# Masks on VectorE, reciprocals left in PSUM and keys copied by ScalarE in the first attention of a two-layer transformer kernel

## The chip, the cores and the metric
One core of one Trainium2 chip runs the whole program. The metric is device time in microseconds (us) of one execution. Engines: PE is TensorE, DVE is VectorE, ACT is ScalarE, POOL is GpSimd, SP is SyncE; PSUM is the memory that TensorE writes, in banks of 128 partitions by 512 fp32 elements, and SBUF the memory of everything else.

## The reference, cut to what matters
The program is two pre-norm transformer layers over x of shape (2, 512, 512). The change touches only the first attention:

```python
x = x + _L0_attn_ref(_layernorm(x), Wq, Wk, Wv, Wo)    # 32 query heads, 8 key/value heads, head size 16
x = x + _L0_ffn_ref(_layernorm(x), ...)
x = x + _L1_attn_ref(_layernorm(x), ...)               # 32 query heads, 8 key/value heads, head size 128
x = x + _L1_ffn_ref(_layernorm(x), ...)

# inside _L0_attn_ref
scores = einsum('bhqd,bhkd->bhqk', q, k_h) / math.sqrt(HEAD_DIM)
scores = where(causal, finfo.min, scores)
attn = softmax(scores, axis=-1)
ctx = einsum('bhqk,bhkd->bhqd', attn, v_h)
return ctx.transpose(0, 2, 1, 3).reshape(b, t, D_OUT) @ Wo
```

## The kernel before, in words
`program` runs stages one after the other: the projection of the first attention (`project0`), the first attention itself (`attend0`), the first feed forward, the second attention (`attention1`), the second feed forward. In each stage every engine has its own program, written out by hand, and executes it strictly in order; engines wait for each other through counting semaphores.

`attend0` (from L1036) works through 8 units u. A unit is one batch and one pair of key/value heads x = 0, 1 with their HPG = 4 query heads each. In a unit there are four query tiles i = 0 to 3 of 128 queries, which see (i + 1) * 128 keys. The softmax is computed in two passes over the scores.

- **First pass, the maxima.** `scores` (L1158) puts scores of 4, 2, 1 and 1 heads into one PSUM bank for i = 0, 1, 2 and 3 (`S_BANKS = [1, 2, 4, 4]` banks for each x). For each head there is one matmul (L1170), and then one bf16 matmul of the identity with the mask (L1173) adds -1e30 to what lies above the diagonal. Three banks go round (`claim_score` waits for `score_read`). On DVE, `maxima` (L1365) takes the negated row maximum of each bank with a `tensor_reduce` (L1369). `put_maxima` splits the maxima of a query tile into two parts and writes them beside the queries (L1381, L1383). The one-head banks, i = 2 and i = 3, are 16 in a unit and 128 in all.
- **Second pass, the weights.** The queries, now with their maxima, are turned by PE (`turn_queries` with again = 1, L1155) and copied out by DVE (`read_queries`, L1405). `turned_scores` (L1187, with its own mask matmul L1190 on the diagonal) gives keys by queries for four heads at once, minus the maximum; ACT takes the exponential (`exponentials`, L1564) and rounds it to its high part (`high`, L1573); POOL subtracts to get the low part (L1683); `weigh` (L1202, L1203) multiplies both with the values, which carry a column of ones for the row sums, into `cbank`. This is done 20 times in a unit, 160 times in all.
- **Out.** DVE copies `cbank` out (`read_heads`, L1414), PE turns it back into `hbank` (`turn_back`, L1208 on, matmuls L1215), and `take_heads` (L1416) on DVE takes the reciprocals of the row sums into the SBUF tile `rsum` (L1424), copies one half of the result (L1425), adds the other (L1427) and multiplies with the reciprocals (L1432). This is done 32 times. `turn_tile` and `project_tile` make the output projection, in the last units and the tail.
- **Keys.** For each unit PE turns four key tiles into `qkbank` (`turn_keys`, L1139) and DVE copies the two halves of partitions, 64 x 512 each, into `k_rows` (`read_keys`, L1393 and L1394). Its place in the order of DVE is between `read_heads(u, 1)` and `take_heads(u, 1)`. `qkbank` is shared by turned keys, turned queries and turned output tiles, one after the other.

On PE, the order of a unit mixes `scores` of unit u with `turned_scores` and `weigh` of unit u - 1. `turn_keys(u)` stands near the start, then come `weigh`, `turn_back`, `turned_scores` and two `weigh`, then `scores(u, 0, 0, 0)`, which needs the keys. The order on ACT at that place is two `exponentials`, then `high(u, 2, 0, 2)`.

The second attention already has the helper `masked_maximum` (L227). It is one DVE operation that adds the mask from SBUF to the scores in PSUM, writes them back and accumulates the minimum of their negative; in the trace it is two instructions, the operation itself and a read of the accumulator, both at L230:

```python
def masked_maximum(nc, m, bank, n, to):
    scores = bank[:, 0:n]
    return nc.vector.tensor_tensor_reduce(scores, scores, m.mask_w[:, T - n:T], -1.0, LARGE, ALU.add, ALU.min, to)
```

`mask_w` is 128 x 512, zero but for its last 128 columns. The memset that makes these zeros (L1466, the third to signal `zeroed`) stands in `attend0` already.

Of the kernel before, what the change touches and what calls it, by code (L numbers as in the profile page):

```python
# [17 lines left out]
ACT = mybir.ActivationFunctionType  # L18
AX_X = mybir.AxisListType.X

P = 128
# [3 lines left out]
QT = T // P  # L25
NG, HPG = 8, 4
HD0, HD1 = 16, 128
# [1008 lines left out]
def attend0(nc, m, inp):  # L1036
# [4 lines left out]
    X2 = 2  # L1041

    S_BANKS = [1, 2, 4, 4]
    M_ALL = X2 * J_ALL
# [10 lines left out]
    def live(u):  # L1055

        return 0 <= u < NU

    done = m.hand_over()
    with ExitStack() as ctx:  # L1060
# [7 lines left out]
        prob = sb("prob", [P, NE, 512])  # L1068
        p_hi, p_lo = sb("p_hi", [P, NP, 512], F32R), sb("p_lo", [P, NP, 512], F32R)
        head_t = m.raw[:, 4:6, :]  # L1070
        rsum, head_sum = sb("rsum", [P, 2, HPG, X2]), sb("head_sum", [P, HPG, X2, HD0])
        head = sb("head", [P, NT, NG * HPG, HD0])
        raw_wo = head[:, QT:NT, :, :].rearrange("p t h n -> p t (h n)")
        c_hi, c_lo = sb("c_hi", [P, 2, KT, P], F32R), sb("c_lo", [P, 2, KT, P], F32R)
# [37 lines left out]
        def _(pe):  # L1112
# [45 lines left out]
            def scores(u, i, x, bank):  # L1158
                if not live(u):
                    return  # L1160
                per, n = HPG // S_BANKS[i], (i + 1) * P
                if x == 0 and bank == 0:
                    pe.wait_ge(q_read, QT * u + i + 1)
                    if i == 0:
                        pe.wait_ge(keys_read, 2 * (u + 1))
                        if u == 0:
                            pe.wait_ge(zeroed, 2)
                out = claim_score()
                for h in range(per):
                    nc.tensor.matmul(out[:, h * n:(h + 1) * n], q_rows[:, bank * per + h, :], k_rows[:, u % 2, x, 0:n],  # L1170
                                     start=(h == 0), stop=False)
                diagonal = out[:, 0:per * n].rearrange("p (h n) -> p h n", h=per)[:, :, i * P:n]
                nc.tensor.matmul(diagonal, m.ident_b[:, :], m.mask_b[:, :].unsqueeze(1).to_broadcast([P, per, P]),  # L1173
                                 start=False, stop=True).then_inc(scored, 1)
                scored_by[QT * u + i] = count["score"]

            def turned_scores(u, i, x, j):

# [27 lines left out]
            def turn_back(u, i):  # L1206

                if not live(u):  # L1208
                    return
                n = QT * u + i  # L1210
                pe.wait_ge(c_read, n + 1)
                if n >= 1:
                    pe.wait_ge(divided, 3 * n)
                for h in range(HPG):
                    last = nc.tensor.transpose(hbank[:, h * VX:(h + 1) * VX], head_t[0:VX, n % 2, h * P:(h + 1) * P],  # L1215
                                               m.ident[0:VX, 0:VX])
                last.then_inc(backed, 1)
# [138 lines left out]
        def _(dve):  # L1356
# [8 lines left out]
            def maxima(u, i, x, bank):  # L1365
                if not live(u):
                    return
                per, n = HPG // S_BANKS[i], (i + 1) * P
                nc.vector.tensor_reduce(nmax[:, i % 2, bank * per:(bank + 1) * per, x],  # L1369
                                        next_score()[:, 0:per * n].rearrange("p (h n) -> p h n", h=per),  # L1370
                                        AX_X, ALU.max, negate=True).then_inc(score_read, 1)

            def put_maxima(u, i):
# [7 lines left out]
                nc.vector.tensor_copy(heads[:, :, 0], both).then_inc(parted, 1)  # L1381
                dve.wait_ge(parted, 2 * n + 1)
                nc.vector.tensor_tensor(heads[:, :, 1], both, heads[:, :, 0].bitcast(F32), ALU.subtract).then_inc(parted, 1)  # L1383

            def read_keys(u):
                if not live(u):
                    return
                dve.wait_ge(keys_turned, u + 1)
                if u >= 2:
                    dve.wait_ge(t_scored, M_ALL * (u - 1))  # L1390
                elif u == 0:
                    dve.wait_ge(zeroed, 2)
                nc.vector.tensor_copy(k_rows[0:64, u % 2, 0, :], qkbank[0:64, :]).then_inc(keys_read, 1)  # L1393
                nc.vector.tensor_copy(k_rows[64:P, u % 2, 1, :], qkbank[64:P, :]).then_inc(keys_read, 1)  # L1394

            def read_queries(u, i):

# [18 lines left out]
            def take_heads(u, i):  # L1416

                if not live(u):
                    return
                n, t, at = QT * u + i, (u // PAIRS) * QT + i, X2 * HPG * (u % PAIRS)  # L1420
                view = hbank[:, 0:HPG * VX].rearrange("p (h x n) -> p h x n", h=HPG, x=X2)
                s, r = head_sum[:, :, :, :], rsum[:, n % 2, :, :]
                dve.wait_ge(backed, n + 1)
                nc.vector.reciprocal(r, view[:, :, :, HD0]).then_inc(divided, 1)  # L1424
                nc.vector.tensor_copy(s, view[:, :, :, V1:VW]).then_inc(divided, 1)  # L1425
                dve.wait_ge(divided, 3 * n + 2)
                nc.vector.tensor_tensor(s, view[:, :, :, 0:HD0], s, ALU.add).then_inc(divided, 1)  # L1427
                dve.wait_ge(divided, 3 * n + 3)
                if u == PAIRS and i == 0:
                    dve.wait_ge(wo_ready, KT)  # L1430
                to = head[:, t, at:at + X2 * HPG, :].rearrange("p (x h) n -> p h x n", x=X2)
                nc.vector.tensor_tensor(to, s, r.unsqueeze(3).to_broadcast([P, HPG, X2, HD0]), ALU.mult).then_inc(head_ready, 1)  # L1432
# [34 lines left out]
            for u in range(-1, NU + 1):  # L1467
                first = 2 * (u - PAIRS - 1) if u in (PAIRS + 1, PAIRS + 2) else None
                tail = u == NU
                maxima(u, 1, 0, 1)  # L1470
                maxima(u, 1, 1, 0)
                maxima(u, 1, 1, 1)
                put_maxima(u, 1)
                if u == NU - 1:
                    dve.wait_ge(stats_made, QT)
                    next_ln.variances(dve)
                maxima(u, 2, 0, 0)
                maxima(u, 2, 0, 1)
                if first is not None:
                    low(first)  # L1480
                maxima(u, 2, 0, 2)
                maxima(u, 2, 0, 3)
                if tail:
                    low(QT)
                take_heads(u - 1, 2)
                if tail:
                    add_tile(QT)
                    low_row(2)
                    make_row(3)
                    low(QT + 1)  # L1490
                    add_tile(QT + 1)
                    low_row(3)
                    low(QT + 2)
                read_queries(u, 1)
                maxima(u, 2, 1, 0)
                maxima(u, 2, 1, 1)
                maxima(u, 2, 1, 2)
                maxima(u, 2, 1, 3)
                put_maxima(u, 2)
                if first is not None:  # L1500
                    add_tile(first)
                if u == NU - 1:
                    next_ln.inverses(dve)
                    make_row(0)
                maxima(u, 3, 0, 0)
                maxima(u, 3, 0, 1)
                if first is not None:
                    low(first + 1)
                maxima(u, 3, 0, 2)
                maxima(u, 3, 0, 3)  # L1510
                read_heads(u - 1, 3)
                read_queries(u, 2)
                if u == NU - 1:
                    low_row(0)
                    make_row(1)
                maxima(u, 3, 1, 0)
                take_heads(u - 1, 3)
                if tail:
                    add_tile(QT + 2)
                    low(QT + 3)  # L1520
                    low_rank_low()
                    add_tile(QT + 3)
                read_heads(u, 0)
                maxima(u, 3, 1, 1)
                maxima(u, 3, 1, 2)
                maxima(u, 3, 1, 3)
                put_maxima(u, 3)
                if first is not None:
                    add_tile(first + 1)
                if u == NU - 1:  # L1530
                    low_row(1)
                    make_row(2)
                take_heads(u, 0)
                read_queries(u, 3)
                read_heads(u, 1)
                read_keys(u + 1)
                take_heads(u, 1)
                maxima(u + 1, 0, 0, 0)
                maxima(u + 1, 0, 1, 0)
                put_maxima(u + 1, 0)  # L1540
                maxima(u + 1, 1, 0, 0)
                read_heads(u, 2)
                read_queries(u + 1, 0)

        @block.scalar
        def _(act):
            def read_queries(u, i):
                if not live(u):
                    return
                n = QT * u + i  # L1550
# [52 lines left out]
            for u in range(-1, NU + 1):  # L1603
# [40 lines left out]
                high(u, 2, 1, 1)  # L1644
                exponentials(u, 2, 0, 2)
                exponentials(u, 2, 1, 2)
                high(u, 2, 0, 2)
                exponentials(u, 3, 0, 0)
                high(u, 2, 1, 2)
# [847 lines left out]
```

## Time and profile before
| | |
|---|---|
| three runs | 1460.55, 1460.55, 1463.03 us (median 1460.55) |
| profiled execution | 1460.84 us, of which 1459.0 us are the span of the instructions |
| mean granted TensorE clock | 0.985 |
| busy share of the span | PE 93%, DVE 70%, ACT 50%, POOL 47% |
| `attend0` in the profile | from about 71.8 to 372.7 us |
| its keys are turned (L1139) from | 73.3, 108.4, 137.6, 167.1, 196.7, 226.3, 265.6 and 305.1 us |

The last line gives the edges of the units. Busy time of PE is a union of matmuls whose ends are modelled and overlap: a matmul of 512 columns is shown with 0.39 us, while one follows the other every 0.23 us. What an instruction costs in a dense stream is thus read from the distance of the ends (start plus duration) of neighbours, not from its duration. In rows of the timeline the first two numbers are start and duration in us, and a bracket gives the idle time of the engine before it and what ended it.

### The profile page before, as it was taken

To read this page: it belongs to the slowest core of one execution; us is meant where nothing else is said; L and a number is where in the kernel's file an instruction comes from. 1 tells how busy PE (TensorE), PEld (TensorE's weight loads), DVE (VectorE), ACT (ScalarE), POOL (GpSimd) and SP (SyncE) were. 2 spreads that over 40 slices of the span, in tenths; PEclk is the share of its full clock that TensorE was granted. 3 is DMA by queue.
4 is the path that set the end of the run, shared out by engine and by line. 5 is a ranking of instruction groups with operands and counts; after the bars stand their busy time and mean duration, and the time that the engine had idled before them with its cause. 6 is when DMAs were issued, how large, how long until landed. Compare 5 with 4: busy or idle time off the path is not lost. (4 is left out here: it accounts for less than half of the span.)

```text
span 1459.0 us, 20197 instructions
## 1 busy us (share of the span) xinstructions
PE 1359.1 (93%) x6904; PEld 1086.5 (74%) x6904; DVE 1020.4 (70%) x2063; ACT 726.4 (50%) x1574; POOL 685.4 (47%) x533
## 2 busy tenths in 40 slices
PE   4779999988898699999999999999999999699999
PEld 3656666655576588888888888888888887578887
DVE  6769998785757677778777787778877878532322
ACT  2548887676534355444544454545544454243332
POOL 3548887666363544244433543444424431055453
PEclk9989999999999999999999999999999999999999
DMA  3000000100110211011110110101101010043332
GB/s 108 3 28 1 1 1 1 25 6 15 52 36 1 73 30 44 9 36 30 29 38 8 37 37 16 44 15 30 44 15 30 22 44 1 15 107 83 103 93 82
DMA packets 64933, 50.72 MB, mean 35 GB/s; under 512 B 5760, under 2 KB 54272, under 8 KB 64576
## 3 DMA queue, kind: packets, MB, share of 16 engines
q1 hardware_dynamic: 64832, 49.43, 11.9%
q8 instruction: 56, 0.92, 0.3%
q14 instruction: 45, 0.37, 0.1%
HBM read 47.32 MB, written 2.10 MB: 34 GB/s over the span
## 5 line engine op out<-in xcount | busy, mean ns | idle before, releaser
L1683 POOL TENSOR_TENSOR a_p_lo<-a_prob,a_p_hi 128x512 fp32r<-128x512 f32 x160 | 203.8, 1288 | 86.3 <-ACT a_p_hi L1573 84.4
L695 ACT ACTIVATE a_pt_hi<-a_ring 128x512 fp32r<-128x512 f32 x160 | 93.8, 596 | 175.8 <-PE a_ring L402 175.7
L831 POOL TENSOR_TENSOR a_rot_a<-a_rot_a,a_rot_b 128x512 f32<-128x512 f32 x80 | 103.5, 1294 | 139.1 <-DVE a_rot_b L574 139.1
L686 ACT ACTIVATE a_prob<-a_score,a_nmax 128x128 f32<-128x128 f32 (+3 forms) x256 | 132.0, 529 | 57.4 <-DVE a_nmax L539 29.0
L2296 POOL TENSOR_TENSOR f_w_lo<-raw,f_w_hi 128x512 fp32r<-128x512 f32 (+2 forms) x66 | 90.8, 1402 | 142.4 <-ACT f_w_hi L2239 142.3
L340 PE MATMUL a_xo<-h_hi,a_w_hi 128*128 128x512 f32 x384 | 151.2, 394 | 5.3 <-POOL a_w_lo L841 4.2
L342 PE MATMUL a_xo<-h_hi,a_w_lo 128*128 128x512 f32 x384 | 151.1, 393 | 0.0
L341 PE MATMUL a_xo<-h_lo,a_w_hi 128*128 128x512 f32 x384 | 150.4, 392 | 0.0
L836 POOL TENSOR_TENSOR a_p_lo<-a_rot_a,a_p_hi 128x512 fp32r<-128x512 f32 x80 | 103.3, 1292 | 69.4 <-ACT a_p_hi L712 69.4
L556 DVE TENSOR_TENSOR a_pt_lo<-a_ring,a_pt_hi 128x512 fp32r<-128x512 f32 x160 | 108.5, 686 | 33.1 <-ACT a_pt_hi L695 32.1
L1573 ACT ACTIVATE a_p_hi<-a_prob 128x512 fp32r<-128x512 f32 x160 | 99.7, 629 | 45.0 <-PE a_cbank L1203 43.0
L1369 DVE TENSOR_REDUCE a_nmax<-a_score 128x1 f32<-128x512 f32 (+3 forms) x176 | 104.6, 634 | 17.3 <-PE a_score L1173 17.1
L841 POOL TENSOR_TENSOR a_w_lo<-raw,a_w_hi 128x512 fp32r<-128x512 f32 x48 | 63.8, 1332 | 107.0 <-ACT a_w_hi L723 107.0
L550 DVE TENSOR_SCALAR a_prob<-a_prob,a_rinv 128x128 f32<-128x128 f32 (+3 forms) x256 | 104.5, 451 | 4.7
L340 PE MATMUL a_xo<-a_wo_hi,a_c_hi 128*128 128x512 f32 x256 | 103.1, 403 | 1.4 <-DVE a_c_lo L561 1.4
L712 ACT ACTIVATE a_p_hi<-a_rot_a 128x512 fp32r<-128x512 f32 x80 | 50.4, 630 | 104.9 <-POOL a_rot_a L831 104.8
L342 PE MATMUL a_xo<-a_wo_hi,a_c_lo 128*128 128x512 f32 x256 | 100.6, 393 | 0.0
L1564 ACT ACTIVATE a_prob<-a_turned 128x512 f32<-128x512 f32 x160 | 92.6, 588 | 15.9 <-POOL a_p_lo L1683 11.2
L846 POOL TENSOR_TENSOR a_wo_lo<-raw,a_wo_hi 128x512 fp32r<-128x512 f32 x32 | 42.8, 1348 | 122.6 <-ACT a_wo_hi L731 122.6
L341 PE MATMUL a_xo<-a_wo_lo,a_c_hi 128*128 128x512 f32 x256 | 100.3, 392 | 0.0
L340 PE MATMUL a_score<-a_p_hi 128*128 128x128 f32 (+3 forms) x256 | 92.8, 363 | 5.3 <-POOL a_p_lo L836 4.6
L402 PE MATMUL a_ring<-ident,a_prob 128*128 128x128 f32 x640 | 93.6, 273 | 1.3 <-DVE a_prob L550 1.0
(330 smaller groups left out, 3763.8 us busy)
## 6 DMA issues: line engine op xcount, KB each, us to landing
raw<-in_L_gate_up_t SPq DMA_DIRECT2D x40, 256.0 KB, 3.0
raw<-in_L_attn_wq SPq DMA_DIRECT2D x32, 256.0 KB, 2.8
raw<-in_L_attn_wo SPq DMA_DIRECT2D x32, 256.0 KB, 2.7
raw<-in_L_down_t SPq DMA_DIRECT2D x20, 256.0 KB, 2.7
x<-in_L_attn_x SPq DMA_DIRECT2D x4, 512.0 KB, 5.6
raw<-in_L_attn_wk SPq DMA_DIRECT2D x8, 256.0 KB, 2.8
raw<-in_L_attn_wv SPq DMA_DIRECT2D x8, 256.0 KB, 2.8
out<-x SPq DMA_DIRECT2D x8, 256.0 KB, 2.5
```

What stands on the lines that cost most here:

```text
L340: nc.tensor.matmul(out, l_hi, r_hi, start=start, stop=False)
L341: nc.tensor.matmul(out, l_hi, r_lo, start=False, stop=False)
L342: return nc.tensor.matmul(out, l_lo, r_hi, start=False, stop=stop)
L550: last = nc.vector.tensor_scalar(pr, pr, rinv[:, i % 2, h:h + 1], None, ALU.mult)
L556: nc.vector.tensor_tensor(pt_lo[:, n % NPT, :], ring[n % 2][:, :], pt_hi[:, n % NPT, :].bitcast(F32), ALU.subtract).then_inc(ring_read, 1)
L686: nc.scalar.activation(prob[i % 2][:, h, 0:n], score[e % NS][:, (h % per) * n:(h % per + 1) * n], ACT.Exp, bias=nmax[:, i % 2, h:h + 1], s ...
L695: nc.scalar.activation(pt_hi[:, n % NPT, :], ring[n % 2][:, :], ACT.Copy).then_inc(pt_hi_done, 1)
L831: nc.gpsimd.tensor_tensor(rot_a[:, c % 2, :], rot_a[:, c % 2, :], rot_b[:, c % 2, :], ALU.add).then_inc(summed, 1)
L836: nc.gpsimd.tensor_tensor(p_lo[:, u % 2, c, :], rot_a[:, c % 2, :], p_hi[:, u % 2, c, :].bitcast(F32), ALU.subtract).then_inc(p_ready, 1)
L1369: nc.vector.tensor_reduce(nmax[:, i % 2, bank * per:(bank + 1) * per, x], next_score()[:, 0:per * n].rearrange("p (h n) -> p h n", h=per), ...
L1573: nc.scalar.activation(p_hi[:, mm % NP, :], prob[:, mm % NE, :], ACT.Copy).then_inc(p_hi_done, 1)
L1683: nc.gpsimd.tensor_tensor(p_lo[:, mm % NP, :], prob[:, mm % NE, :], p_hi[:, mm % NP, :].bitcast(F32), ALU.subtract).then_inc(p_ready, 1)
```

## The change
1. In `scores`, a bank of one head gets no mask matmul: its only matmul starts and stops the bank. In `maxima`, such a bank is read with `masked_maximum` in place of `tensor_reduce`; before the first of them DVE waits for the third memset.
2. In `take_heads`, the reciprocals are written in place, over the sums in `hbank` (PSUM), and the multiplication reads them from there. `rsum` goes. `turn_back` on PE waits for the multiplication of the tile before (`head_ready`), since the bank is now read until then, where it waited for the addition.
3. `read_keys` moves from DVE to ACT as two ACTIVATE copies of 64 x 512, placed between `exponentials(u, 2, 1, 2)` and `high(u, 2, 0, 2)`.

```diff
-        rsum, head_sum = sb("rsum", [P, 2, HPG, X2]), sb("head_sum", [P, HPG, X2, HD0])
+        head_sum = sb("head_sum", [P, HPG, X2, HD0])
...
                 out = claim_score()
+                scored_by[QT * u + i] = count["score"]
+                if per == 1:
+                    nc.tensor.matmul(out[:, 0:n], q_rows[:, bank, :], k_rows[:, u % 2, x, 0:n], start=True,
+                                     stop=True).then_inc(scored, 1)
+                    return
                 for h in range(per):
...
-                scored_by[QT * u + i] = count["score"]
...
                 if n >= 1:
-                    pe.wait_ge(divided, 3 * n)
+                    pe.wait_ge(head_ready, n)
...
                 per, n = HPG // S_BANKS[i], (i + 1) * P
+                if per == 1:
+                    if u == 0 and i == 2:
+                        dve.wait_ge(zeroed, 3)
+                    masked_maximum(nc, m, next_score(), n, nmax[:, i % 2, bank, x:x + 1]).then_inc(score_read, 1)
+                    return
...
-                s, r = head_sum[:, :, :, :], rsum[:, n % 2, :, :]
+                s, r = head_sum[:, :, :, :], view[:, :, :, HD0]
                 dve.wait_ge(backed, n + 1)
-                nc.vector.reciprocal(r, view[:, :, :, HD0]).then_inc(divided, 1)
+                nc.vector.reciprocal(r, r).then_inc(divided, 1)
...
                 read_heads(u, 1)
-                read_keys(u + 1)
                 take_heads(u, 1)
...
         @block.scalar
         def _(act):
+            def read_keys(u):
+                if not live(u):
+                    return
+                act.wait_ge(keys_turned, u + 1)
+                if u >= 2:
+                    act.wait_ge(t_scored, M_ALL * (u - 1))
+                elif u == 0:
+                    act.wait_ge(zeroed, 2)
+                nc.scalar.activation(k_rows[0:64, u % 2, 0, :], qkbank[0:64, :], ACT.Copy).then_inc(keys_read, 1)
+                nc.scalar.activation(k_rows[64:P, u % 2, 1, :], qkbank[64:P, :], ACT.Copy).then_inc(keys_read, 1)
...
                 exponentials(u, 2, 0, 2)
                 exponentials(u, 2, 1, 2)
+                read_keys(u + 1)
                 high(u, 2, 0, 2)
```

## Rows read from the trace of the kernel before
**Rows 1.** Sums by stretch: us, busy of PE, PEld, DVE, ACT, POOL, PE clock, DMA.
```profile
73.30:108.40 35.10, 26.33 (x125) 17.47 (x126) 23.47 (x44) 16.54 (x29) 15.05 (x13) 0.83 0.08 29
...
196.70:226.30 29.60, 29.30 (x176) 19.57 (x175) 26.62 (x57) 24.24 (x45) 25.49 (x21) 1.00 0.00 1
226.30:265.60 39.30, 36.55 (x208) 25.11 (x207) 30.58 (x63) 25.64 (x47) 25.52 (x21) 1.00 0.00 1
...
305.10:335.10 30.00, 27.35 (x151) 18.31 (x151) 24.65 (x59) 22.85 (x40) 21.07 (x18) 0.94 0.00 1
335.10:372.70 37.60, 29.00 (x137) 19.65 (x137) 19.44 (x41) 21.62 (x38) 21.47 (x17) 0.95 0.05 14
```
**Rows 2.** Waits from 108.4 to 226.3 us (units 1 to 4): us, times, longest.
```profile
POOL a_p_lo L1683 <- ACT a_p_hi L1573: 14.1, 28, 1.1
...
PE a_qkbank L1155 <- DVE h_lo L1383: 0.8, 3, 0.3
```
**Rows 3.** Timeline of PE in unit 3, 512 keys: masks and what follows.
```profile
184.69 0.23 PE L1173 MATMUL a_score<-mask_b,ident_b 128*128 128x128 bf16 x1
...
185.05 0.23 PE L1173 MATMUL a_score<-mask_b,ident_b 128*128 128x128 bf16 x1
...
185.09 0.43 PE L1202 MATMUL a_cbank<-a_p_hi,vw 128*66 128x512 f32 x1
...
185.36 0.39 PE L1203 MATMUL a_cbank<-a_p_lo,vw 128*66 128x512 f32 x1
```
**Rows 4.** Timeline of PE in unit 3, 384 keys: two successive masks.
```profile
182.01 0.23 PE L1173 MATMUL a_score<-mask_b,ident_b 128*128 128x128 bf16 x1
...
182.32 0.23 PE L1173 MATMUL a_score<-mask_b,ident_b 128*128 128x128 bf16 x1
```
**Rows 5.** Timeline of PE in the second attention: 384-column matmuls that need no mask.
```profile
563.29 0.34 PE L340 MATMUL a_score<-a_p_hi 128*128 128x384 f32 x1
563.47 0.34 PE L341 MATMUL a_score<-a_p_lo,a_p_hi 128*128 128x384 f32 x1
```
**Rows 6.** Timeline of DVE in unit 3: runs of plain maxima.
```profile
182.03 1.94 DVE L1369 TENSOR_REDUCE a_nmax<-a_score 128x1 f32<-128x384 f32 x4
...
184.60 1.89 DVE L1369 TENSOR_REDUCE a_nmax<-a_score 128x1 f32<-128x512 f32 x3 [0.22 <-PE a_score L1173]
```
**Rows 7.** Timeline of DVE in the second attention: ends of two successive masked maxima.
```profile
626.92 0.14 DVE L230 DVE_READ_ACCUMULATOR2_ANT a_nmax<- 128x1 f32 x1
...
627.57 0.14 DVE L230 DVE_READ_ACCUMULATOR2_ANT a_nmax<- 128x1 f32 x1
```
**Rows 8.** The tile head_sum: shortest, median and longest ns, first and last start.
```profile
L1427 DVE TENSOR_TENSOR a_head_sum<-a_hbank,a_head_sum x32: 291/291/293, 103.5 to 368.6; 128x128 f32<-128x128 f32 x32
L1432 DVE TENSOR_TENSOR a_head<-a_head_sum,a_rsum x32: 291/726/1325, 103.8 to 368.9; 128x128 f32<-128x128 f32 x32
```
**Rows 9.** Timeline around the copy of the keys for unit 3.
```profile
167.82 0.60 ACT L1564 ACTIVATE a_prob<-a_turned 128x512 f32<-128x512 f32 x1 [0.31 <-POOL a_p_lo L1683]
...
167.84 0.68 DVE L1393 CAST a_k_rows<-a_qkbank 64x512 fp32r<-64x512 f32 x1 [0.15 <-PE a_qkbank L1139]
...
168.55 0.69 DVE L1394 CAST a_k_rows<-a_qkbank 64x512 fp32r<-64x512 f32 x1
...
169.77 0.56 PE L1170 MATMUL a_score<-a_k_rows,a_q_rows 128*128 128x128 f32 x4
...
172.91 1.30 POOL L1683 TENSOR_TENSOR a_p_lo<-a_prob,a_p_hi 128x512 fp32r<-128x512 f32 x1 [1.05 <-ACT a_p_hi L1573]
...
173.30 0.40 PE L1202 MATMUL a_cbank<-a_p_hi,vw 128*66 128x512 f32 x1
```
**Rows 10.** Timeline of ACT in unit 3: two successive copies of 512 elements.
```profile
176.88 1.14 ACT L1573 ACTIVATE a_p_hi<-a_prob 128x512 fp32r<-128x512 f32 x2
```
**Rows 11.** Waits from 305.1 to 335.1 us (unit 7): us, times, longest.
```profile
PE a_score L1170 <- DVE a_nmax L1369: 2.2, 2, 1.8
DVE n1a_y L106 <- ACT n1a_sd L160: 1.9, 1, 1.9
```

More of the change, by code:

```diff
@@ L1383, in put_maxima @@
                 nc.vector.tensor_tensor(heads[:, :, 1], both, heads[:, :, 0].bitcast(F32), ALU.subtract).then_inc(parted, 1)
[L1385 to L1394, printed above, removed]
             def read_queries(u, i):
```

## Prediction, made before the changed kernel was run
> **What bounds the kernel now.** The change lies in one stage of 301 us, so I cut that stage into its units, at the times when the keys are turned, and read the busy time by stretch. In unit 4, as in units 1 to 3, PE is busy 29.30 of 29.60 us; DVE has 26.62, POOL 25.49, ACT 24.24 [rows 1]. The waits of units 1 to 4 say the same: PE idles 0.8 us in three of the four units, for the split of the maxima on DVE, while the largest wait of all is POOL's, 14.1 us for ACT [rows 2]. So in four units PE is the bound, and what leaves its stream is gained as long as nobody else becomes late. Units 5 and 6 take 39.3 us each because they carry output projections; PE idles 2.7 us in one. Unit 7 has 2.65 us of idle PE. In unit 0 and in the tail PE idles 8.8 and 8.6 us: they are chains of several engines [rows 1].
>
> **The masks, PE's side.** 16 mask matmuls leave each unit, 128 in all. What one costs in the stream is read from ends. Two banks of 512 keys end, with their masks, at 184.92 and 185.28, 0.36 apart; a matmul of 512 columns alone (the low `weigh`, 185.75 after 185.52) takes 0.23, so the mask costs 0.13 [rows 3]. For 384 keys the ends are 182.24 and 182.55, 0.31 apart [rows 4], against 0.18 for a matmul of 384 columns that has no mask behind it [rows 5]: 0.13 again. Where a `weigh` follows, the mask costs less: that `weigh` ends 0.24 after the mask [rows 3], its usual 0.23, and only about 0.07 is left, the mask's own stretch. I take 0.075 there. By the order of PE, 9 of the 16 masks are followed by a score matmul and 7 by a `weigh` or a transposition: 9 x 0.13 + 7 x 0.075 = 1.70 us in a unit. The bounds are 16 x 0.07 = 1.1 and 16 x 0.13 = 2.1.
>
> The Trainium skill (TensorE: Matmul & The Clock Gate, Back-to-back issue gap) states N / 2.4 + 2.5 ns for an isolated matmul, an estimate of 56 ns for 128 columns. By that a unit would gain 0.9 us, and the rival "own stretch only" below would have it all; the trace has 0.13 where another score matmul follows.
>
> **The masks, DVE's side.** Maxima of 384 elements come every (1.94 - 0.55) / 3 = 0.46 us, of 512 every (1.89 - 0.69) / 2 = 0.60 [rows 6]; the masked form of 512 ends every 0.65 (627.71 after 627.06), its accumulator read included [rows 7]. That is 0.05 more for each, 0.8 us in a unit.
>
> **The reciprocals.** The addition at L1427, with one input in PSUM, takes 291 to 293 ns all 32 times. The multiplication at L1432, of the same size and with both inputs in SBUF, takes 291 at best, 726 as median and 1325 at most [rows 8]. With its second input in PSUM it has the form of L1427. The bounds are thus 0.29 and 0.73; I take 0.29, since the nearest row has it without spread: 4 x 0.43 = 1.7 us less DVE in a unit. The Trainium skill (SBUF — State Buffer, SBUF: two separate sides) speaks of a lock, by which a VectorE operation with two SBUF inputs waits out a GpSimd operation; by it 0.29 is right, without it 0.73 could stay. No other price hangs on it. Writing eight reciprocals to PSUM in place of SBUF I cost between -0.05 and +0.05, and take 0. The later wait of `turn_back` costs nothing: the tile before was multiplied some us earlier, in every unit.
>
> **The keys.** DVE starts at 167.84 and ends at 169.24 [rows 9], so it loses 1.4 us in a unit. ACT gains two copies. Two of 128 x 512 come (1.14 - 0.62) = 0.52 apart [rows 10]; I take 1.1 for the pair, between 1.0 and 1.3. In the old times: ACT's exponential ends at 168.42, so the copies would end at 169.5. The first score matmul starts at 169.77 [rows 9]. So PE hardly waits, with about 0.3 to spare. Behind the copies on ACT stand `high(u, 2, 0, 2)` and what POOL makes of it, all 1.1 us later. POOL has the room: it sat idle for 1.05 before 172.91, so it had ended the second of that pair at 171.86, and its `weigh` starts at 173.30 [rows 9], 1.4 later. This cover shrinks to about 0.3; what is late next, if it is gone, is that `weigh`.
>
> **Load afterwards.** In a unit DVE goes to 26.6 + 0.8 - 1.7 - 1.4 = 24.3, ACT to 25.3, POOL stays at 25.5, PE needs 29.6 - 1.7 = 27.9. PE stays the bound, but POOL would be at 91%, and the split of the maxima, which PE already waited for, has DVE shorter by less than PE. I take off 0.25 for new stalls (bounds 0 and 0.8): 1.45 us gained in each of units 1 to 4.
>
> **The sum.** Units 1 to 4: 4 x 1.45 = 5.8. Units 5 and 6: the same, and some of 2.7 us of idle PE shrinks with a shorter DVE, 1.9 each, 3.8. Unit 7: PE waits 2.2 us for maxima and DVE 1.9 for ACT's square root [rows 11]; the part behind that root gains no masks, so 1.2. Unit 0: only the masks of i = 2 stand in its chain (8 x 0.12 = 1.0), and the new copies sit on an ACT that PE waits for, so 0.7. The tail: shorter multiplications, 0.4. Together 11.9 us. The profiled execution took 1460.84 us (span 1459.0 and 1.8 around it), 0.3 above the median of the three runs. That gives 1448.9; I say 1449.0. The stages behind attention are only moved forward.
>
> **Rivals.**
> - *More than that (0.12).* All eight units gain 1.7 (13.6), and the PE idle of units 5 to 7 shrinks by another 4: 17.6 less, 1443.2. For it: `weigh` starts 1.4 us behind POOL even in the tighter pair. Against it: unit 0 is not bound by PE.
> - *A mask is worth only its own stretch (0.11).* Then a unit gains 16 x 0.07 = 1.1, less the 0.25, and all come to 8 x 0.85 = 6.8: 1454. Against it stand the 0.13 of two sizes.
> - *POOL's chain holds the unit (0.10).* The hole that the copies make on ACT is passed on to POOL, which is idle 4.1 us in a unit now, always for ACT. If its idle time in a unit ends at 3.7, the unit ends at 29.2 and gains 0.4: 3.3 in all, 1457.5, half of it within what can be told from no change. Against it: the later gap of 1.05 should take up the hole.
> - *Slower (0.05).* The keys are late: ACT reaches the copies only after `exponentials(u, 2, 1, 2)`, and PE stands before `scores(u, 0, 0, 0)`. That costs as soon as the copies end 0.3 later than the old 169.5, and decides the sign from 2.0 later on (1.7 + 0.3). At 2.5 later every unit loses 0.5: 4 us more, 1465. For it: ACT waits for POOL at that place already, 0.31 [rows 9]. Against it: POOL would have to be over a whole operation later.
>
> **How the numbers follow.** The forecast has 0.62. A difference within 0.2%, 2.9 us, cannot be told from none. Faster: 0.62 + 0.12 + 0.11 and half of POOL's 0.10, 0.90; same: 0.06, slower: 0.04. The range goes from the upper rival, 1443.0, past "own stretch" to 1455.5, and leaves out POOL's rival and the slower one, 0.15. The bounds of the forecast's own terms, masks 1.1 to 2.1 and stalls 0 to 0.8 in a unit, lie mostly within it.
>
> **What would show it.** In the changed profile, keys should be turned every 28.1 us in units 1 to 4, and unit 5 and 6 take 37.4. L1432's successor should be 0.29 us without spread, the masked maxima end 0.65 and 0.51 apart, DVE be busy under 25 in a unit. The waits should show PE still hardly idle, with less than 0.6 us in a unit. I am wrong if PE idles over 1 us in a unit, at the first score matmul (keys), at a `weigh` (POOL) or at the second turning of the queries (DVE), or if the unit shrinks by 1.1 with PE dense.

## The result and the profile after

The changed kernel takes 1460.3 us, median of 20 runs (1456.1 to 1462.2), against 1464.0 for the kernel before (median of 20, 1460.6 to 1465.8). The ratio is 0.9973, 95% interval 0.9966 to 0.998: by it the kernel is 3.9 us faster, a third of the 11.9 forecast. Its profiled execution took 1458.99 us, with a span of 1457.1. Runs of the kernel before spread over 5 us, and the profiled one of 1460.84, on which the forecast was built, lies at their lower end. Of the 35 runs of the kernel before that stand beside e1 to e4, those with a mean granted clock of 0.985 or 0.986 took 1460.1 to 1461.4 us, those with 0.981 or 0.982 took 1463.6 to 1465.9; the profiled one had 0.985. So 3 us of the absolute miss are the base, and the ratios are what counts below; 0.001 is 1.46 us.

Sums by stretch of the changed kernel, cut where keys are turned (us, then busy time of PE, PEld, DVE, ACT, POOL, the granted TensorE clock, and DMA), against [rows 1]:

```profile
73.70:108.10 34.40, 26.25 (x108) 17.32 (x109) 22.33 (x58) 18.24 (x32) 15.44 (x13) 0.80 0.09 31
108.10:138.40 30.30, 28.74 (x160) 20.51 (x159) 25.20 (x70) 25.25 (x47) 26.06 (x21) 0.96 0.01 2
...
167.50:196.70 29.20, 27.64 (x160) 19.61 (x159) 25.64 (x71) 25.18 (x48) 25.32 (x20) 1.00 0.00 1
...
226.00:263.50 37.50, 34.90 (x192) 24.77 (x191) 27.92 (x77) 26.02 (x49) 24.35 (x20) 1.00 0.00 1
...
301.70:331.70 30.00, 25.03 (x133) 17.25 (x132) 23.58 (x66) 23.25 (x41) 20.57 (x17) 0.94 0.01 1
331.70:370.50 38.80, 29.97 (x142) 20.05 (x140) 19.46 (x50) 22.79 (x40) 22.43 (x18) 0.96 0.05 14
```

Unit 3 (from 167.5 us) has 27.64 us of PE where unit 4 before had 29.30: the forecast 1.7 us have left its stream. But it lasts 29.2, not 27.9. 1.5 us are now idle, all in one place, the second turning of the queries. The waits of units 1 to 4, to be read against [rows 2] (PEld is the loading of weights, ahead of the matmul itself):

```profile
PE a_qkbank L1155 <- DVE h_lo L1392: 4.5, 3, 1.5
...
PEld a_score L1171 <- DVE a_nmax L230: 1.3, 4, 0.3
```

The first is the idle time; the second does not show as idle PE, and the section on why the prediction was wrong comes back to it. The timeline at the first (start, duration):

```profile
185.87 10.25 POOL L1692 TENSOR_TENSOR a_p_lo<-a_prob,a_p_hi 128x512 fp32r<-128x512 f32 x8 [0.39 <-ACT a_p_hi L1581]
...
192.31 0.14 DVE L230 DVE_READ_ACCUMULATOR2_ANT a_nmax<- 128x1 f32 x1
...
192.48 1.02 DVE L1390 CAST h_lo<-a_nmax 128x8 fp32r<-128x8 f32 x1
...
192.57 0.71 PE L1191 MATMUL a_turned<-a_q_max,a_k_rows 128*128 128x512 f32 x2
...
193.54 1.19 DVE L1392 TENSOR_TENSOR h_lo<-a_nmax,h_lo 128x8 fp32r<-128x8 f32 x1
...
194.78 0.66 PE L1155 MATMUL a_qkbank<-ident,h_lo 128*128 128x128 f32 x4 [1.50 <-DVE h_lo L1392]
```

and the same place before, on DVE and on POOL:

```profile
191.39 1.87 DVE L1369 TENSOR_REDUCE a_nmax<-a_score 128x1 f32<-128x512 f32 x3
193.30 0.18 DVE L1381 CAST h_lo<-a_nmax 128x8 fp32r<-128x8 f32 x1
193.51 1.18 DVE L1383 TENSOR_TENSOR h_lo<-a_nmax,h_lo 128x8 fp32r<-128x8 f32 x1
```

```profile
186.56 6.39 POOL L1683 TENSOR_TENSOR a_p_lo<-a_prob,a_p_hi 128x512 fp32r<-128x512 f32 x5 [0.74 <-ACT a_p_hi L1573]
193.37 2.53 POOL L1683 TENSOR_TENSOR a_p_lo<-a_prob,a_p_hi 128x512 fp32r<-128x512 f32 x2 [0.42 <-ACT a_p_hi L1573]
```

DVE reads the last maxima at 192.45. Then it splits them (`put_maxima`), a copy and a subtraction on 8 elements for each partition. They take 0.17 to 0.18 us where nothing stops them; here the copy takes 1.02 and the subtraction 1.19, and PE, which stood ready at 193.28, starts at 194.78. Both read and write SBUF, and POOL runs eight operations without a gap over that time. Before, POOL had a gap of 0.42 us at 192.95, the copy went through it, and only the subtraction waited. The new wait takes back 1.2 us of what the masks gave.

The other planned steps are there. The masked maxima of 512 and of 384 keys end 0.65 and 0.51 us apart, as forecast. The multiplication of `take_heads` (shortest, median, longest ns), against [rows 8]:

```profile
L1430 DVE TENSOR_TENSOR a_head<-a_head_sum,a_hbank x32: 286/286/290, 103.3 to 366.7; 128x128 f32<-128x128 f32 x32
```

DVE is busy for 25.6 us in a unit where the load sum said 24.3; in e9 below, where nothing makes it wait for POOL, it is 24.41.

Unit 7 and the tail became 1.2 us longer, with PE waiting 4.3 us in unit 7 where it waited 2.2 [rows 11]:

```profile
PE a_score L1171 <- DVE a_nmax L230: 4.3, 2, 2.2
```

And unit 1 is 1.0 us longer than before: its clock is 0.96 in the rows above, with a stretch of 3.4 us at half clock (1.2 GHz) from 107.1 to 110.5 that the profiled run before does not have. In the 3.4 us ahead of that stretch PE was busy for 1.4 us.

### The profile page after: what moved, and what is told of

Its sections match the earlier page's. It is cut to its first block and busy times, and to the rows that moved or that the text cites. A ratio compares the mean times of both kernels' runs of the same rounds, so it can differ in the third digit from the quotient of the medians.

```text
span 1457.1 us, 20077 instructions
## 1 busy us (share of the span) xinstructions
PE 1350.4 (93%) x6776; PEld 1086.6 (75%) x6776; DVE 1010.8 (69%) x2175; ACT 735.0 (50%) x1590; POOL 684.2 (47%) x533
## 5 line engine op out<-in xcount | busy, mean ns | idle before, releaser
L686 ACT ACTIVATE a_prob<-a_score,a_nmax 128x128 f32<-128x128 f32 (+3 forms) x256 | 132.2, 530 | 57.2 <-DVE a_nmax L539 28.9
L230 DVE CUSTOM_DVE_ANT_0 a_score<-a_score,mask_w 128x512 f32<-128x512 f32 (+1 forms) x256 | 155.3, 642 | 5.7 <-PE a_score L1171 5.4
```

The source lines that it names most:

```text
L686: nc.scalar.activation(prob[i % 2][:, h, 0:n], score[e % NS][:, (h % per) * n:(h % per + 1) * n], ACT.Exp, bias=nmax[:, i % 2, h:h + 1], s ...
```

## The experiments

A unit's length is the median of units 2 to 4 in the profile; "idle" is idle PE in one of them, waits over 0.15 us alone. "Splits" are the copy and subtraction of the maxima; "in PSUM" says that they read a PSUM bank (e4 explains how). e1, e2, e3, e8 and e10 are built up from the kernel before, the others are changes to the changed kernel.

| kernel | ratio to before | 95% interval | unit, us | idle, us |
|---|---|---|---|---|
| before | 1 | | 29.56 | 0.27 |
| changed | 0.9973 | 0.9966 to 0.998 | 29.16 | 1.50 |
| masks alone (e1) | 1.0015 | 1.0006 to 1.0025 | 30.02 | 1.5 |
| reciprocals alone (e2) | 0.9969 | 0.9959 to 0.998 | 29.22 | 0.26 |
| keys alone (e3) | 1.0006 | 0.9996 to 1.0016 | 29.55 | 0.26 |
| changed, one split in PSUM (e4) | 0.9986 | 0.9975 to 0.9998 | 29.54 | 0.5 to 1.2 |
| changed, all splits in PSUM (e5) | 0.9946 | 0.9932 to 0.996 | 28.67 | 0.68 |
| masks, reciprocals (e6) | 0.9946 | 0.9932 to 0.9961 | 29.13 | 1.50 |
| masks, reciprocals, splits (e7) | 0.992 | 0.9906 to 0.9934 | 27.91 | 0.23 |
| reciprocals, splits (e8) | 0.9955 | 0.9941 to 0.9968 | 28.72 | 0 |
| e5, keys one place earlier (e9) | 0.9919 | 0.9906 to 0.9933 | 27.92 | 0.22 |
| masks, splits (e10) | 0.9986 | 0.9976 to 0.9997 | 29.21 | 0.76 |
| e7, square root earlier (e11) | 0.9925 | 0.9912 to 0.9938 | 27.93 | 0.23 |
| changed, keys one place earlier (e12) | 1.0006 | 0.9997 to 1.0015 | 30.56 | 2.42 |

**The three parts alone.** e1, e2 and e3 are the kernel before with one part of the change each; all three together are the changed kernel.

```diff
 # e1: the masks, on PE and then on DVE
+                if per == 1:
+                    nc.tensor.matmul(out[:, 0:n], q_rows[:, bank, :], k_rows[:, u % 2, x, 0:n], start=True,
+                                     stop=True).then_inc(scored, 1)
+                    return
...
+                if per == 1:
...
+                    masked_maximum(nc, m, next_score(), n, nmax[:, i % 2, bank, x:x + 1]).then_inc(score_read, 1)
 # e2: the reciprocals
-                s, r = head_sum[:, :, :, :], rsum[:, n % 2, :, :]
+                s, r = head_sum[:, :, :, :], view[:, :, :, HD0]
...
 # e3: the keys, from DVE to ACT
                 read_heads(u, 1)
-                read_keys(u + 1)
                 take_heads(u, 1)
...
                 exponentials(u, 2, 1, 2)
+                read_keys(u + 1)
```

> The masks' part alone (one-head banks masked on VectorE; reciprocals and keys as before). Theory S (the split of the last maxima on VectorE waits behind GpSimd's operations and gives the gain back): PE busy falls by 1.6 to 1.7 us in a unit, PE's idle time before the second turning of the queries (L1155 <- DVE, 0.27 us before, 1.50 in the changed kernel) rises to 1.0 to 1.5, units 1 to 4 take 29.0 to 29.4 us, and the time falls by 2 to 4 us. Theory K (it is the copies of the keys on ScalarE that close the gaps in GpSimd's stream, so that the split finds none): without them the split keeps its gap, the idle stays near 0.3, units take 28.0 to 28.3 and the time falls by 9 to 12 us. Theory C (the TensorE clock: the added half-clock stretches near 107 and 469 us take the gain): units 2 to 4 are short here as well, and only stretches at half clock are long.

> The reciprocals' part alone. PE bounds units 1 to 4 and no mask leaves it, so every theory expects units of 29.5 to 29.6 us there. The multiplication in take_heads should take 0.29 us without spread in place of 0.73. Some of the idle PE of units 5 to 7 and the tail may go: 0 to 3 us less in all. Theory S expects no change in the idle before the second turning of the queries (0.27).

> The keys' part alone: copies by ScalarE, masks and reciprocals as before. PE bounds the units, so 29.5 to 29.7 us in units 1 to 4 and the time within 2 us of before. Theory K expects GpSimd's run of operations at the split to be unbroken and PE's idle time at the second turning of the queries to rise from 0.27 to over 1 us, so units over 30 us and the time 4 to 8 us longer. Theory S expects the idle at 0.2 to 0.6.

Measured: the masks alone make the kernel slower, 1.0015. One unit of their profile, and their multiplications in `take_heads`, which keep both inputs in SBUF:

```profile
171.40:201.50 30.10, 28.33 (x159) 19.49 (x159) 28.28 (x73) 24.16 (x45) 25.56 (x21) 1.00 0.00 1
```

```profile
L1441 DVE TENSOR_TENSOR a_head<-a_head_sum,a_rsum x32: 291/868/1331, 103.9 to 373.3; 128x128 f32<-128x128 f32 x32
```

PE is down from 29.3 to 28.3 us, and the unit is longer than before. The idle at the split is 1.5 without the copies on ACT, so theory K falls, and with long units at full clock theory C too. DVE is at 28.3 us, because its multiplications wait longer too, 868 ns in the median where it was 726 [rows 8]. Theory S expected a gain here and missed that second wait. With the reciprocals in PSUM as well (e6), the unit goes from 30.02 to 29.13.

The reciprocals alone give as much as the whole change, 0.9969, against every expectation for units 1 to 4: 29.2 us in place of 29.6, with the masks all there.

```profile
170.20:199.40 29.20, 28.92 (x176) 19.61 (x175) 25.70 (x57) 24.33 (x45) 25.47 (x21) 1.00 0.00 1
```

The idle time is unchanged; the 0.3 us are in PE's busy time, which falls from 29.3 to 28.9. Comparing the ends of its matmuls one by one, two places differ. The first `weigh` behind the turned keys ended 0.45 us after its neighbour before, 0.23 here; it waits for `cbank` to be copied out. And the first turning of the keys ended 0.24 after its neighbour before, 0.11 here; it waits for the queries to be copied out of `qkbank`. Both copies stood on DVE behind a slow multiplication (0.73 us, from 195.32 in the timeline before), and the two waits, 0.35 us together, are not listed as idle. Units 5 and 6 are 1.4 and 1.3 us shorter. The keys alone change nothing that can be told (1.0006, units of 29.55), as expected by theory S and against theory K.

**The splits in PSUM.** e4 takes the supposed cause away: the maxima are first copied into the score bank that DVE has just read, and both operations of the split read them there. PE's next user of that bank waits for the split (not shown in the cut below). e4 does so for i = 3 only, e5 for all four tiles.

```diff
                 dve.wait_ge(score_read, count["score"])
+                if i == 3:                       # e4; e5: always
+                    spare = score[(count["score"] - 1) % NS][:, 0:X2 * HPG]
+                    spread_count[0] += 1
+                    nc.vector.tensor_copy(spare, both).then_inc(spread, 1)
+                    dve.wait_ge(spread, spread_count[0])
+                    both = spare
                 nc.vector.tensor_copy(heads[:, :, 0], both).then_inc(parted, 1)
```

> The changed kernel, with the split of the last maxima (i = 3) made from PSUM: the maxima are first copied into the score bank just read, and both operations of the split read them there, so that neither has two SBUF inputs nor copies SBUF to SBUF. Theory S: the three operations take 0.6 to 0.8 us where the two took 2.25, PE's idle time there falls from 1.50 to 0 to 0.3, units 2 to 4 take 27.8 to 28.3 us, and the time is 6 to 10 us under the changed kernel's, 10 to 13 under before. Theory K: the same here. Theory C: the units shorten, but new stretches at half clock appear and less than half of that is left. If the split was never what PE waited for, nothing changes.

> The changed kernel with all four splits of a unit's maxima made from PSUM, not only the one of i = 3. Theory P (VectorE operations with two SBUF inputs, or SBUF copies, wait out GpSimd's operations, in whichever split meets one): with only i = 3 mended the wait went to the splits of i = 0 and 1, 1.2 to 1.3 us in three of four units, with 0.73 us of idle PE behind it. With all four mended, every split takes under 0.7 us, units 1 to 4 all take 28.0 to 28.4 us and only the idle before the first score matmul (keys, 0.5) is left: 1.5 to 4 us less than with i = 3 alone, 4 to 8 under before. Rival, the TensorE clock: the units shorten, and new stretches at half clock eat it, so the time stays at the changed kernel's within 1 us.

e4 at the place that was mended:

```profile
186.59 11.51 POOL L1706 TENSOR_TENSOR a_p_lo<-a_prob,a_p_hi 128x512 fp32r<-128x512 f32 x9 [0.39 <-ACT a_p_hi L1595]
...
193.20 0.17 DVE L1401 COPY a_score<-a_nmax 128x8 f32<-128x8 f32 x1
...
193.41 0.17 DVE L1404 CAST h_lo<-a_score 128x8 fp32r<-128x8 f32 x1
193.61 0.17 DVE L1406 TENSOR_TENSOR h_lo<-a_score,h_lo 128x8 fp32r<-128x8 f32 x1
...
193.84 0.66 PE L1159 MATMUL a_qkbank<-ident,h_lo 128*128 128x128 f32 x4
```

Under one unbroken run of nine POOL operations the three small ones take 0.17 us each, 0.58 from the start of the first to the end of the last, and PE has no idle time. But the time is no lower than the changed kernel's, 0.9986 against 0.9973. The unit was now in another phase to POOL, and the other splits met its operations (the subtraction; shortest, median, longest ns):

```profile
L1406 DVE TENSOR_TENSOR h_hi<-a_nmax,h_hi x8: 173/695/1325, 80.3 to 178.2; 128x8 fp32r<-128x8 f32 x8
...
L1406 DVE TENSOR_TENSOR h_lo<-a_score,h_lo x4: 171/172/172, 102.3 to 193.6; 128x8 fp32r<-128x8 f32 x4
```

`h_hi` holds the split maxima of i = 0 and 1 of the first four units, still made in SBUF: up to 1325 ns. The mended one, `h_lo<-a_score` (i = 3), takes 171 to 172. Unit 3, where no subtraction was hit, took 28.2 us; units 1, 2 and 4, where two were, took 29.5 to 29.8. With all of them mended (e5), units 1 to 4 take 28.7 to 28.8, more than the 28.0 to 28.4 expected, and the time is 0.9946, within the 4 to 8 us expected.

That it is POOL that holds DVE up can be read from all the traces at once. Nine of them (before, changed, e1 to e4, e6, e10, e12) still have DVE operations of this kind with all operands in SBUF: copies and subtractions of the split, and multiplications of `take_heads`. 213 of these 624 take over 0.06 us longer than undisturbed. Every one of the 213 ends as if it had started 0.135 to 0.145 us before the recorded end of a POOL operation. The same operations with an operand in PSUM started 429 times while a POOL operation was running, over all traces, and none took more than 4 ns longer. No run took POOL's work away.

**The keys.** In e5, 0.5 us of idle PE are left before the first score matmul. e6 and e7 put the keys back on DVE.

> Masks and reciprocals, the keys still copied by VectorE. The keys' part alone cost 0 to 1.5 us. If the copies on ScalarE only add 0.3 to 0.5 us of idle PE before the first score matmul of a unit, this is 1 to 3 us faster than the changed kernel, PE idle at the split still about 1.5 us. If taking the copies off VectorE is what the rest of the gain rests on, it is slower than the changed kernel by 1 to 3 us.

> Masks and reciprocals, keys on VectorE, all splits from PSUM. Theory P: PE is the bound again in units 1 to 4 with under 0.3 us of idle time, units of 27.6 to 28.1 us, the lowest time of all: 8 to 12 us under before. Clock rival: 3 to 5 us under before only, with more stretches at half clock.

Both are the changed kernel but for the keys, e7 with e5's splits as well:

```diff
                 read_heads(u, 1)
+                read_keys(u + 1)
                 take_heads(u, 1)
...
                 exponentials(u, 2, 1, 2)
-                read_keys(u + 1)
```

e6 (0.9946) is 3.9 us faster than the changed kernel, more than the 1 to 3 expected, though its units 2 to 4 are no shorter and idle as long. In the profiles, the stretch from unit 7 to the last matmul of the output projection takes 72.2 us in the changed kernel and 69.2 in e6, where the splits of unit 7 were not hit (0.17 to 0.18 us each, against up to 1.32), and unit 1 of e6 lacks the stretch at half clock. Behind that, the same code took 1083.2 and 1086.1 us: e6's trace has two more stretches of 3.4 us at half clock there. So profiles of two kernels can differ by 3 us in code that is the same.

e7, one unit:

```profile
164.00:191.90 27.90, 27.60 (x159) 19.53 (x158) 25.58 (x77) 23.92 (x45) 25.35 (x21) 1.00 0.00 1
```

e7 is 11.7 us faster than before (0.992), with the keys on DVE. That this is the forecast's size is a coincidence of terms, as the next section shows. The keys on ACT cost 0.76 us in a unit (e5 against e7), and 0.73 of it is one step between the ends of two matmuls, at the first score matmul behind the keys. The timeline of e5 shows why:

```profile
165.42 0.60 ACT L1586 ACTIVATE a_prob<-a_turned 128x512 f32<-128x512 f32 x1
165.47 0.38 PE L1143 MATMUL a_qkbank<-ident,f_lo 128*128 128x128 f32 x2
...
166.47 0.60 ACT L1586 ACTIVATE a_prob<-a_turned 128x512 f32<-128x512 f32 x1 [0.45 <-POOL a_p_lo L1706]
...
166.96 0.58 ACT L1566 ACTIVATE a_k_rows<-a_qkbank 64x512 fp32r<-64x512 f32 x1
...
167.56 0.59 ACT L1567 ACTIVATE a_k_rows<-a_qkbank 64x512 fp32r<-64x512 f32 x1
...
168.26 0.63 PE L1181 MATMUL a_score<-a_k_rows,a_q_rows 128*128 128x128 f32 x4 [0.49 <-issue]
```

The keys are turned at 165.85, but an exponential stands ahead of the copies on ACT, and it waits for POOL until 166.47. So the copies end at 168.15 and PE starts at 168.26, after 0.49 us of idle time. e9 puts them one place earlier:

```diff
+                read_keys(u + 1)
                 exponentials(u, 2, 1, 2)
-                read_keys(u + 1)
```

> As e5 (the changed kernel, all splits from PSUM), but ScalarE copies the keys before exponentials(u, 2, 1, 2), which waits for GpSimd, not behind it. In e5 a unit takes 28.67 us against 27.93 with the keys on VectorE, and 0.47 of that is idle PE before the first score matmul. Theory L (the copies are late because ScalarE stands behind that exponential): the idle 0.47 goes, units 1 to 4 take 28.0 to 28.3 us, and the time is 2 to 4 us less than e5's. Rival (ScalarE is too full wherever they stand, and the work behind them on GpSimd comes late): units stay at 28.6 to 29, with the idle time moved to a weigh or an exponential.

```profile
163.81 0.60 ACT L1586 ACTIVATE a_prob<-a_turned 128x512 f32<-128x512 f32 x1
...
164.28 0.58 ACT L1566 ACTIVATE a_k_rows<-a_qkbank 64x512 fp32r<-64x512 f32 x1
...
164.89 0.59 ACT L1567 ACTIVATE a_k_rows<-a_qkbank 64x512 fp32r<-64x512 f32 x1
...
165.99 0.56 PE L1181 MATMUL a_score<-a_k_rows,a_q_rows 128*128 128x128 f32 x4
```

Now the copies end at 165.48, before PE asks for them, and e9 (0.9919) equals e7. Theory L (the copies are late because of their place on ACT) holds.

e12 makes the same move in the changed kernel, with its splits in SBUF.

> The changed kernel as it is, its splits in SBUF, with the copies of the keys one place earlier on ScalarE, before exponentials(u, 2, 1, 2). The same kernel with keys on VectorE (e6) has ratio 0.9946 to before, the changed kernel 0.9973. If the late place of the copies makes that difference, this comes to 0.993 to 0.996, about 2 to 4 us under the changed kernel, with PE still idle 1.5 us in a unit behind the split (units 29.1), and with the stall of unit 7 (2.1 us at the first one-head bank in the changed kernel, 0.9 in e6) back near 0.9. If the copies on ScalarE cost as such, it stays at 0.997.

It gained nothing: 1.0006, 4.8 us slower than the changed kernel, and both expectations missed. The subtraction of its splits:

```profile
L1392 DVE TENSOR_TENSOR w_both<-a_nmax,w_both x12: 174/1214/1234, 208.6 to 328.9; 128x8 fp32r<-128x8 f32 x12
L1392 DVE TENSOR_TENSOR h_hi<-a_nmax,h_hi x8: 173/1212/1216, 79.8 to 183.1; 128x8 fp32r<-128x8 f32 x8
L1392 DVE TENSOR_TENSOR h_lo<-a_nmax,h_lo x8: 174/682/6109, 90.7 to 199.8; 128x8 fp32r<-128x8 f32 x8
```

Now the subtractions of three splits in each unit meet a POOL operation, where one did, and the unit takes 30.56. Unit 0 is 4 us longer as well; the 6.11 us are there. The same move is worth -3.9 us (e5 to e9, 0.9946 to 0.9919) with free splits and +4.8 with blocked ones. While the splits are blocked, an edit can be worth more by what it does to their phase against POOL than by the work that it moves.

**What masks and reciprocals are worth once the splits are free.**

> Reciprocals and all splits from PSUM, mask matmuls kept, keys on VectorE. Theory P: the idle of 0.27 us before the second turning of the queries goes and units 1 to 4 take 28.9 to 29.0 us, 0.3 under the reciprocals alone, so 5 to 8 us under before. Against the kernel of masks, reciprocals and such splits the difference is what 128 mask matmuls are worth once VectorE isn't blocked: 1.0 to 1.4 us in a unit.

> Masks and all splits from PSUM; the multiplication in take_heads keeps both inputs in SBUF, keys on VectorE. Theory P: the splits are short, but the multiplications wait for GpSimd, 0.7 to 0.9 us in place of 0.29, and PE stalls behind them (in e1: the first weigh after the keys, 0.2, and a turning of queries, 0.24). Units 1 to 4 take 28.3 to 28.7 us, the time 2 to 5 us over e7. If the reciprocals' part is worth nothing once the splits are free, units take 27.9 as in e7.

Against e7, e8 has the mask matmuls and plain maxima back, and e10 the reciprocals in SBUF:

```diff
-                if per == 1:
...
-                    masked_maximum(nc, m, next_score(), n, nmax[:, i % 2, bank, x:x + 1]).then_inc(score_read, 1)
...
-                s, r = head_sum[:, :, :, :], view[:, :, :, HD0]
+                s, r = head_sum[:, :, :, :], rsum[:, n % 2, :, :]
```

One unit of e8:

```profile
168.70:197.30 28.60, 28.60 (x175) 19.63 (x174) 25.27 (x61) 24.09 (x45) 25.37 (x21) 1.00 0.01 2
```

e8 has no idle PE at all; 28.7 us, less than the 28.9 to 29.0 expected, is the stream with its mask matmuls. Against e7's 27.9 the masks are worth 0.8 us in a unit, less than the 1.0 to 1.4 expected. e10, without the reciprocals, takes 29.2, not the 28.3 to 28.7 expected, and is 9.7 us slower than e7: with masked maxima on DVE the slow multiplications cost 1.3 us in a unit, where they cost 0.3 to 0.4 before.

**Unit 7.** e11 is e7 with the square root moved on ACT to the start of unit 7.

```diff
                 high(u - 1, 3, 1, 3)
+                if u == NU - 1:
+                    next_ln.roots(act)
...
-                if u == NU - 1:
-                    next_ln.roots(act)
```

> e7 (masks, reciprocals, all splits from PSUM, keys on VectorE) with the square root of the next layer norm, and its two table loads, moved on ScalarE from behind high(7, 0, 0, 0) to the start of unit 7. In e7 VectorE waits 1.44 us for it and PE 1.93 us behind VectorE. If that wait is what stops PE there, the 1.9 go and the time is 1 to 2 us less than e7's. If the table loads only delay the exponentials of unit 7 in its place, it is the same or up to 2 us more.

0.9925, the same as e7 within the intervals. The wait of PE moved from DVE's maxima to ACT's copy of the queries (2.8 us), which stands behind the two table loads: the second case.

## Why the prediction was wrong

- **The step that failed is the allowance for new stalls,** "I take off 0.25 for new stalls (bounds 0 and 0.8)". Measured by the ends of matmuls, unit 3 of the changed kernel has about 1.6 us of new stalls, twice the upper bound. 1.23 of them are at the place that the prediction named last, "at the second turning of the queries (DVE)", and show as idle PE, 1.50 where it was 0.27. The other 0.34 are hidden in busy time: the fifth score matmul of 384 keys ends 0.51 us after its neighbour where two such neighbours end 0.17 to 0.18 apart, because it waits for a bank that DVE reads with a masked maximum. The bound was too low because it was taken from the wait before, 0.27, as if it were a slack that shrinks. [Rows 2] show that wait, and the timeline of before shows why it was short: one of two blocked operations had found a gap of POOL. The prediction treated the lock between DVE and POOL for the multiplication only, and wrote that "No other price hangs on it". The splits, with all operands in SBUF, hung on it, and PE waits for them. e4, e5 and e7 show it: with the splits in PSUM and the same masks the wait is gone.
- **The masks.** Their price on PE was right to the last term. Between the ends of e2 and of the changed kernel, nine masks are worth 0.12 to 0.13 each and seven 0.07 to 0.08, 1.7 us in a unit (three of the nine stand before a `turned_scores` and not, as the prediction has it, before a score matmul). So the rival "own stretch only" is out, and so are the 56 ns estimated from the Trainium skill (TensorE: Matmul & The Clock Gate, Back-to-back issue gap). But in e7 the masks are worth 0.8 only (against e8), because two score matmuls come late by 0.34 and 0.46: the one above, and one whose bank still holds the split that e7 itself puts there, of which 0.23 show as idle.
- **The size of e7 is luck.** Its unit is 1.65 us shorter than before, where the forecast had 1.45 for the masks less the stalls. By the ends, 0.8 of it are the masks; 0.35 are two waits that the reciprocals removed, and 0.48 is the old wait at the split, 0.27 of it listed as idle, which the splits in PSUM removed. Neither of the last two was in the forecast.
- **The reciprocals.** 0.29 without spread was right. That they spare DVE time and nothing else was wrong: they alone bring 4.5 us (e2), 0.3 to 0.4 in each steady unit and 1.3 to 1.4 in units 5 and 6. The rule of the Trainium skill (SBUF — State Buffer, SBUF: two separate sides) is that a VectorE operation in a two-port mode or with two SBUF inputs and a GpSimd operation exclude each other, and whichever starts first goes first. All but one of the 213 slowed operations agree with it; the 6.11 us of e12 do not, a wait that lasted for five GpSimd operations. The first half of the rule could cover the copy of the split, 1.02 us, which the prediction overlooked; in which mode that copy runs no trace shows.
- **The keys.** "So PE hardly waits" holds for the changed kernel, but for a reason that was not forecast: PE was held up behind the split first, and nothing showed (29.16 us a unit, and 29.13 in e6). e3 showed nothing either (29.55). Once PE ran freely (e5) the keys cost 0.76 a unit. The slower rival's mechanism was there, with 0.5 us of idle time where the sign would have needed 2, since ACT stands behind POOL at that place.
- **Units 5 to 7, unit 0 and the tail.** Units 5 and 6 gained 1.8 and 1.3 (forecast 1.9 each), but the reciprocals alone give 1.4 and 1.3 there (e2), so the sizes came out near by luck. Unit 0 gained 0.7 (0.7); no run isolates its terms. Unit 7 and the tail lost 1.2 where 1.6 was forecast as a gain: in unit 7 the subtractions of i = 0 and i = 1 took 1.32 and 1.22 us, and PE waited 4.3. In e6, with the keys on DVE and these splits not hit, PE waited 3.1, and unit 7 and the tail were 1.8 us shorter than before.
- **The sum.** By the turning of the last keys 3.4 us were gained, 2.2 were left at the end of the stage, and 1.9 in the whole span. Two half-clock stretches that the profile before lacks (unit 1, and at 468.9 us behind the stage) go with 1.0 and 0.3 us of that. How such stretches come and go between runs was not isolated.

## What to carry to other kernels

Before an engine off the critical path is made faster or fuller, list which of its operations can be blocked by another engine, and which of those the bound engine waits for; two operations of 0.17 us with their operands in SBUF took 2.2 us beside a busy GpSimd. Moving the operands to PSUM, even with one more copy, removed the wait here. A short wait in a trace can be a blocked operation that found a gap, so bound it by the longest case of its kind (here a whole GpSimd operation for each such instruction, and once five), not by what it shows. Read a "busy" matmul stream by the distances of its ends, since waits of 0.1 to 0.3 us hide there. And where a total agrees with a forecast, check the terms: in e7 it agreed for the wrong ones.

## What was not expected of the hardware

- A plain copy of 8 fp32 elements for each partition from SBUF to SBUF is blocked as the subtraction is: 1.02 us for 0.17. Copy and subtraction each wait out an operation, one after the other.
- The wait can last for more than one operation: in e12 a subtraction of unit 0 took 6.11 us (the longest of `h_lo` above), while GpSimd worked off five operations, of two kinds in turn at first, without a gap. In units 1 to 4 no subtraction of a split took over 1.32.
- The masks moved to DVE made a unit longer by 0.46 us (e1), though PE was the bound and lost 1.7 us of work by the ends of its matmuls: over 2 us of waits took its place.
